# Interleaving the high and low parts of three split tiles, element by element

## The reference, cut to what matters

```python
x = x + _L0_xattn_ref(_layernorm(x), ctx, ctx, Wq, Wk, Wv, Wo)   # q = query @ Wq ... return out @ Wo
x = x + _L0_ffn_ref(_layernorm(x), weight, bias, lora_A, lora_B, lora_start_indices)
x = x + _L1_xattn_ref(_layernorm(x), ctx, ctx, Wq, bq, Wk, bk, Wv, bv, 16)   # K = k @ Wk.T + bk
x = x + _L1_ffn_ref(_layernorm(x), W_base, b_base, enc0, enc1, coefs0, coefs1, mask0, mask1)
```

## Time and profile before

| what | value |
|---|---|
| median of 3 runs | 294.1 us (293.99 to 294.46) |
| span of the profiled execution, first to last instruction | 292.5 us |
| that execution's own time apart from its span | not recorded; the median run is 1.6 us above the span |
| TensorE busy (matmuls) | 284.9 us, 97% |
| TensorE weight loads, beside them | 224.2 us, 77% |
| VectorE, ScalarE, GpSimd busy | 234.3, 167.4 and 146.6 us |

### The profile page before, as it was taken

The page is one execution under the profiler, slowest core; times in us unless marked ns, Lnnn a source line. Parts: engine busy times, 40 slices in busy tenths (PEclk is TensorE's granted clock), DMA queues, the critical chain, the costliest instruction groups (busy, mean ns, idle before and its releaser), DMA issues.

```text
span 292.5 us, 6282 instructions
## 1 busy us (share of the span) xinstructions
PE 284.9 (97%) x2136; PEld 224.2 (77%) x2136; DVE 234.3 (80%) x358; ACT 167.4 (57%) x284; POOL 146.6 (50%) x194
## 2 busy tenths in 40 slices
PE   7999999999999999999999999999999998999996
PEld 2689676856784675788988998989977687888875
DVE  5589987779978966665778868899977999998752
ACT  5965868876488398834445454466444475343310
POOL 6594332061414048504304661696097879875742
PEclk9999999999999999999999999999999999999999
DMA  7987454757377542490332515225635321000222
GB/s 224 348 224 277 147 210 146 242 182 256 90 252 233 170 128 94 148 255 20 103 100 51 135 26 131 57 60 145 172 107 156 109 72 38 2 0 3 108 89 92
DMA packets 35784, 39.52 MB, mean 135 GB/s; under 512 B 3928, under 2 KB 21848, under 8 KB 35754
## 3 DMA queue, kind: packets, MB, share of 16 engines
q1 hardware_dynamic: 35754, 39.13, 43.9%
HBM read 20.48 MB, written 6.29 MB: 92 GB/s over the span
## 4 chain that ended last, share of the span: by engine, by line
PE 81%; DVE 7%; POOL 4%; issue 3%; ACT 2%; DMA 1%; POOLq 0%; DVEq 0%; ACTq 0%
PE ps L494 16%; PE ps L496 15%; PE ps L495 15%; PE ps L783 5%; PE ps L693 5%; PE ps L859 4%; PE ps L750 3%; PE ps L772 3%; PE ps L898 3%; PE ps L871 2%; PE ps L796 1%; PE ps L909 1%; DMA out<-XB 1%; PE ps L706 1%; DVE xn L1225 1%
## 5 line engine op out<-in xcount | busy, mean ns | idle before, releaser
L1464 POOL TENSOR_TENSOR slot_l<-stg,slot_h 128x512 fp32r<-128x512 f32 x19 | 25.3, 1343 | 41.9 <-ACT slot_h L967 41.9
L1260 DVE TENSOR_REDUCE mx<-ps 128x8 f32<-128x1024 f32 x32 | 38.1, 1214 | 2.5 <-PE ps L750 2.2
L494 PE MATMUL ps<-xT_h,slot_h 128*128 128x256 f32 x128 | 36.9, 288 | 0.0
L496 PE MATMUL ps<-xT_h,slot_l 128*128 128x256 f32 x128 | 36.0, 281 | 0.0
L495 PE MATMUL ps<-xT_l,slot_h 128*128 128x256 f32 x128 | 35.9, 281 | 0.0
L1046 ACT ACTIVATE PT<-ps 128x1024 f32<-128x1024 f32 x32 | 31.2, 1026 | 4.2 <-PE ps L772 4.1
L1476 POOL TENSOR_SCALAR var_eps<-moments 128x1 f32<-128x1 f32 x32 | 7.5, 235 | 41.8 <-DVE moments L1221 40.9
L1506 POOL TENSOR_TENSOR zpart<-P 128x512 f32<-128x512 f32 x16 | 21.2, 1323 | 10.8 <-ACT P L1123 9.8
L1123 ACT ACTIVATE P<-ps 128x1024 f32<-128x1024 f32 x16 | 16.4, 1025 | 17.0 <-PE ps L871 17.0
L494 PEld LDWEIGHTS ps<-xT_h,slot_h 128*128 128x128 f32 x128 | 24.2, 189 | 1.7 <-issue 0.4
L992 ACT ACTIVATE xT_h<-ps 128x512 fp32r<-128x512 f32 x24 | 14.1, 600 | 18.3 <-PE ps L693 15.4
(11 more groups left out here) (175 smaller groups left out, 853.4 us busy)
## 6 DMA issues: line engine op xcount, KB each, us to landing
ctx_in<-in_ctx SPq DMA_DIRECT2D x20, 256.0 KB, 3.0
QS<-Q_h SPq DMA_DIRECT2D x16, 256.0 KB, 3.3
o_dram<-OTs SPq DMA_DIRECT2D x16, 256.0 KB, 2.2
Q<-Q1d SPq DMA_DIRECT2D x64, 64.0 KB, 2.1
X<-in_x SPq DMA_DIRECT2D x8, 256.0 KB, 5.4
stg<-in_wq SPq DMA_DIRECT2D x8, 256.0 KB, 5.1
QS<-Q_l SPq DMA_DIRECT2D x8, 256.0 KB, 3.2
O<-o_dram SPq DMA_DIRECT2D x8, 256.0 KB
```

The costliest lines, as they stand in the source:

```text
L494: eng.matmul(dst, left[0], right[0], start=start, stop=False)
L496: return eng.matmul(dst, left[1], right[0], start=False, stop=stop)
L1260: dve.tensor_reduce(mx[:, b % 2, :].rearrange("p (x r) -> p r x", r=REP)[:, r, :], wide(step).rearrange("p k (g t) -> p (k g) t", g=4), AX ...
L1464: pool.tensor_tensor(lo, src, hi.bitcast(F32), ALU.subtract).then_inc(w_lo_pool, 1)
```

## The change

The high and the low tile of slot 0, of OT and of fT become one tile each, with an innermost dimension of 2; the names `_h` and `_l` become views of it. An element's high part and its low part lie side by side, 4 bytes each, and two neighbouring elements of one part lie 8 bytes apart instead of 4. Every instruction stays, with the same shapes, in the same order; the memory used is the same.

```diff
-            slot_h[0] = sb("slot0_h", [C, D], F32R, short)
-            slot_l[0] = sb("slot0_l", [C, D], F32R, short)
+            slot0 = sb("slot0", [C, D, 2], F32R, short)
+            slot_h[0], slot_l[0] = slot0[:, :, :, 0], slot0[:, :, :, 1]
...
-            OT_h, OT_l = s1("OT_h", [C, P], F32R), s1("OT_l", [C, P], F32R)
-
-            fT_h, fT_l = s1("fT_h", [C, 2, P], F32R), s1("fT_l", [C, 2, P], F32R)
+            OT = s1("OT", [C, P, 2], F32R)
+            OT_h, OT_l = OT[:, :, :, 0], OT[:, :, :, 1]
+
+            fT = s1("fT", [C, 2, P, 2], F32R)
+            fT_h, fT_l = fT[:, :, :, :, 0], fT[:, :, :, :, 1]
```

## The result

The changed kernel took 298.63 us (median of 4 runs, 298.6 to 298.95), the one before, run beside it, 294.05 (4 runs). The ratio is 1.0164, with a 95% interval from 1.0143 to 1.0186: **slower by 4.6 us, or 1.6%**. Forecast were 294.1 us and a range up to 298.2, so the time lies 0.4 us outside.

What follows compares the result with a forecast made beforehand. TensorE, busy 284.9 of 292.5 us, was taken to bound the kernel. Loads, adapter and splits at 0 each left the 292.5 us span plus 1.6 us around it: 294.1 us, range 293.2 to 298.2.

Steps and rivals of the forecast that it cites:

- the adapter's moving operand: The adapter's 32 matmuls stream fT with gaps; bounds 0 to +3.8 us, taken as 0.
- The rival at half speed: The adapter's 32 matmuls stream interleaved fT at half speed, 118 ns more each: +3.8 us, 297.9 us; chance 0.15.
- 8 bytes is a sixteenth: Reason for 0 at the adapter: 128-byte jumps cost ScalarE a factor of 1.94, and 8 bytes is a sixteenth of that.
- Weight loads: Loads from slot 0, OT and fT step 8 bytes per column; bounds -3.0 to +42.1 us, taken as 0.
- 81 ns of latency: Part of a 128-column weight load's 189 ns that the next load overlaps; the columns take the other 108 ns.
- The sweep argument: Interleaved loads sweep 9.5 bytes per ns, packed moving operands already 8.7, so weight loads cost 0.
- from 10 ns more per load: Point where the load rival decides: at 256 moving columns a load has 117.7 - 108 = 10 ns to spare.
- the load rival: Weight loads bound the 384 matmuls of 256 columns: full +42.1 us (336.2), partial +13.5 (307.6); chance 0.13.
- Splits: ScalarE writes the high half with gaps, VectorE and GpSimd read it; at most +9.2 us, taken as 0; slower-splits rival 297.2, chance 0.11.
- the 0.3 us of room: At the start, last GpSimd split ends at 16.89 us, first matmul needing it starts at 17.19.
- Pace lower: Matmuls settle at the lower start-to-start times seen, 113 and 227 ns: half of 3.0 us gained, 292.6 us; chance 0.11.
- The adapter's 297.9: Time in us forecast if the adapter streams at half speed: 294.1 + 3.8; chance 0.15.

## Why the prediction was wrong

**The step that failed** is the adapter's moving operand: "I take 0, with less trust than for the loads". It measured +3.49 us in the trace and +3.3 us alone. The rival at half speed had the mechanism and nearly the size (109 ns per matmul where it said 118), at a chance of 0.15. The reason given for 0 was that "8 bytes is a sixteenth" of the jump that costs ScalarE a factor of 1.94. That took the length of a jump for the price. The runs show it isn't: 8, 12, 16 and 32 bytes all cost half the speed, and 512 bytes in turn cost nothing. A clue for the right number stood in the same paragraph: the stream would have had to sweep 17.4 bytes per ns, "twice what any row shows". But that would have been luck, since bytes per ns are not the limit: with 16-byte steps the same matmul swept 4096 bytes in 232 ns, 17.7 per ns, and with 32-byte steps twice that. What the runs show in its place is that the stream halves where the lines of 16 bytes aren't used in whole.

**Weight loads.** The 0 came out nearly right: with 8-byte steps 197 ns instead of 189, so 116 instead of 108 for 128 columns (with the prediction's 81 ns of latency taken off), a 7% surcharge rather than a factor. The sweep argument behind it fits 16-byte steps as well (2048 bytes in 234 ns, 8.8 per ns) but not 32-byte steps (4096 bytes in 246 ns, 16.6 per ns), so as a mechanism it isn't shown. And "from 10 ns more per load" was too generous a point of decision. 8 ns more moved the pace from 117.7 to 120 ns, 4 ns longer than the load itself. Here the mechanism of the load rival was right in the smallest measure: the matmuls of Q0 and K1 took some 1.3 us more in the trace, the two waits not counted, and slot 0 alone costs 0.9 us net. At 512 columns it was right that the load is nearly free (OT alone: 1.0001).

The prediction weighed the Trainium skill, page "SBUF — State Buffer", section Specifications (TRN2): two hits per 16-byte line give full bandwidth. For weight loads the runs agree to within some 5%: two elements per line 194 to 198 ns against 188, one per line 309 to 335. For the moving operand they differ: two elements per line run at half speed (229 ns against 118), and one per line is no slower (217 to 233); the measurement decides.

**Splits.** Forecast 0; nearly true for OT (median 702 ns on VectorE against 694 before) and for fT (685 against 683), although ScalarE's writes grew by 5 to 9% (632 to 688, 593 to 647). At the start it was wrong: the two GpSimd splits took 0.65 us more, above the bound of 0.54 that the prediction set, used up the 0.3 us of room that it had named, and left a wait of 0.28 us.

**Pace lower.** It was there, in the 512-column steps WO and F0 (233 to 230 ns), as a small refund and not as the outcome. With fT alone and with OT alone the steps that read them have it too; F1 with xT interleaved went the other way, from 227 to 233.

**The range.** Each rival was priced as if it came alone. The adapter's 297.9 was nearly the upper end, with 0.3 us on top for the pace; slot 0's 0.9 us had no room beside it. Rivals that don't exclude each other add up, and here two did: fT alone cost 3.3 us and slot 0 alone 0.9, which from 294.05 makes 298.3 of the 298.6 measured. The sum is good to some half a microsecond and no better, since without fT the change cost 1.9 us and not 0.9.

## What to carry to other kernels

Interleave two parts of a matmul operand only where it is the stationary one and the matmul behind the load is long enough to hide it (here 512 columns: nothing to be measured with OT and fT, some 4 ns each in F1 with xT; 256: some 3 ns each). A moving operand wants its 16-byte lines used in whole, so keep each fp32r part packed, or check that every layout that serves one reader doesn't halve another: fT was harmless as weights in F0 and cost 3.5 us as the stream of LT. Before choosing between "no cost" and "half speed" for an access that no row shows, put a small run of that access beside the forecast, or leave both values in the range: here neither the length of the jump nor the bytes per ns told which it would be.

## What the runs showed of the hardware that was not expected

- A moving fp32r operand of 256 columns takes 110 to 127 ns (135 to 141 for the first behind a slow one) where all of each 16-byte line is read soon after each other (packed, packed one element later, four of eight on the lines, two places 512 bytes apart in turn), and 200 to 240 where it isn't (steps of 8, 12, 16 and 32 bytes, two of four, four of eight across the lines, sixteen places in turn). Four places in turn lie between, at 140. Whether one or two elements of a line are used makes little difference.
- Weight loads of 128 columns behave otherwise: packed 187 to 191 ns, 8-byte steps 194 to 198, 16-byte steps 309 to 330, 32-byte steps 327 to 335. (Ahead of a moving operand at half speed packed ones show 201 to 208.)
- ScalarE's write of 512 fp32r elements from PSUM goes like the loads: 593 ns packed, 643 with 8-byte steps, 1121 with 16, 1164 with 32. So does VectorE's subtraction behind it: 683, 685, 1096, 1170.
- GpSimd's subtraction, with its source read in jumps, went from 1620 to 1920 ns when its other operands got 8-byte steps, while the same with a sequential source stayed at 1308 against 1296. VectorE's, of which there is one with jumps, went from 1451 to 1755 and stayed at 694 against 691. Why gaps cost there and not with a sequential source is open.
